# First expert results handed to the second picks' rows, sums scattered straight to the output, dispatch scatters of the attention stage spread

## What is computed

```
logits = xf @ gate_w.T                      # 8192 x 8
top_p, top_i = top_k(softmax(logits), 2)
w = top_p / (sum(top_p) + 1e-9)
capacity = int(1.25 * T / E)                # 1280 rows for each expert and pick
rank = the token's place among those that picked this expert with this pick
y = down(silu(gate(x)) * up(x))             # only where rank < capacity
out = x + w0 * y0 + w1 * y1                 # a pick over capacity adds nothing
```

## Time and profile before

| | |
|---|---|
| median of 3 runs (lowest, highest) | 1113.87 us (1110.75, 1114.72) |
| profiled execution: its time, its span | 1111.77 us, 1110.0 us |
| mean granted TensorE clock | 0.888 |
| busy share: PE, DVE, POOL, ACT | 84%, 55%, 48%, 42% |
| linear attention | 0 to about 280 us |
| cross-attention and routing | about 280 to 803 us, last batch's exponentials at 758 us |
| experts | 804 to 1085 us |
| loading, adding and storing the second picks | 1085 to 1110 us |
| `DMA_INDIRECT` of the attention (L842), of the experts (L1603) | 128 x 1.01 us, 160 x 0.98 us |

### The profile page before, as it was taken

The page is one execution under the profiler, slowest core; times in us unless marked ns, Lnnn a source line. Parts: engine busy times, 40 slices in busy tenths (PEclk is TensorE's granted clock), DMA queues, the critical chain, the costliest instruction groups (busy, mean ns, idle before and its releaser), DMA issues.

```text
span 1110.0 us, 26366 instructions
## 1 busy us (share of the span) xinstructions
PE 930.1 (84%) x9107; PEld 656.8 (59%) x9107; DVE 615.1 (55%) x1940; ACT 466.1 (42%) x722; POOL 537.0 (48%) x747
## 2 busy tenths in 40 slices
PE   4799999999899888889888888896189899899860
PEld 3577777776566565556566566665156566666550
DVE  6788888886467665556566566543212222233336
ACT  1365566664455444444444444442033333233320
POOL 2466565665223444443444444444625666555660
PEclk8799999999999987887799798965589999899995
DMA  6379200000000000000000000000023322335418
GB/s 215 98 279 338 85 0 0 0 1 1 2 3 10 18 17 21 15 10 4 7 7 7 9 9 9 9 22 9 13 72 88 96 81 70 96 97 146 121 36 303
DMA packets 48178, 67.25 MB, mean 61 GB/s; under 512 B 12338, under 2 KB 25441, under 8 KB 48088
## 3 DMA queue, kind: packets, MB, share of 16 engines
q1 hardware_dynamic: 36480, 52.65, 14.6%
q0 software_dynamic: 9216, 8.42, 2.7%
q10 hardware_dynamic: 2392, 4.93, 1.1%
HBM read 34.41 MB, written 42.09 MB: 69 GB/s over the span
## 4 chain that ended last, share of the span: by engine, by line
PE 50%; another core or an unknown queue 14%; issue 6%; DVE 3%; POOL 2%; ACT 2%; DMA 2%; POOLq 0%; DVEq 0%; ACTq 0%; SPq 0%
PE psum L1709 9%; PE psum L1286 8%; PE psum L1272 7%; PE psum L1721 5%; PE psum L1306 5%; PE psum L1260 2%; PE psum L1289 2%; PE psum L1314 2%; DVE Y L1635 1%; PE psum L625 1%; PE psum L1256 1%; PE psum L1703 1%; POOL dispatched L842 1%; PE psum L605 1%
## 5 line engine op out<-in xcount | busy, mean ns | idle before, releaser
L1603 POOL DMA_INDIRECT expert_out<-yo,token x160 | 156.5, 978 | 124.5 <-issue 107.2
L842 POOL DMA_INDIRECT dispatched<-z,idx x128 | 129.0, 1008 | 101.3 <-DVE idx L1027 53.9
L1185 ACT ACTIVATE PT<-psum,key_bias 77x2048 f32<-77x2048 f32 x64 | 125.6, 1962 | 123.0 <-PE psum L1289 112.9
L1646 DVE TENSOR_TENSOR h<-psum,act_g 128x512 f32<-128x512 f32 x80 | 53.5, 689 | 185.4 <-PE psum L1709 105.9
L918 DVE TENSOR_REDUCE top_score<-psum 128x8 f32<-128x616 f32 x128 | 101.8, 795 | 42.6 <-PE psum L1272 38.9
L1286 PE MATMUL psum<-qT,Kb 32*77 32x128 f32 x2048 | 105.6, 326 | 18.6 <-ACT MT L1198 17.5
L1272 PE MATMUL psum<-Kb,qT 32*128 32x308 f32 x512 | 110.1, 508 | 0.8 <-issue 0.5
L1709 PE MATMUL psum<-xT,gate 128*128 128x512 f32 (+1 forms) x192 | 82.9, 564 | 17.5 <-ACT xT L1666 9.2
L1286 PEld LDWEIGHTS psum<-qT,Kb 32*77 32x77 f32 x2048 | 72.8, 173 | 32.0 <-issue 31.2
L1681 ACT ACTIVATE act_g<-psum 128x512 f32<-128x512 f32 x80 | 46.0, 596 | 96.4 <-PE psum L1709 29.6
L1721 PE MATMUL psum<-down,h 128*128 128x128 f32 x640 | 80.8, 280 | 5.1 <-DVE h L1646 5.1
(11 more groups left out here) (169 smaller groups left out, 1766.7 us busy)
## 6 DMA issues: line engine op xcount, KB each, us to landing
dispatched<-zeros SPq DMA_DIRECT2D x40, 258.0 KB, 2.7
xin<-dispatched SPq DMA_DIRECT2D x40, 258.0 KB
expert_out<-zeros SPq DMA_DIRECT2D x32, 256.0 KB, 2.1
X<-in_x SPq DMA_DIRECT2D x16, 256.0 KB, 2.7
yb<-expert_out SPq DMA_DIRECT2D x16, 256.0 KB
Y<-expert_out SPq DMA_DIRECT2D x7, 512.0 KB, 7.9
out<-Y ACTq DMA_DIRECT2D x7, 512.0 KB, 6.6
expert_out<-yo,token POOLq DMA_INDIRECT x160
```

Source lines behind the costliest of these rows:

```text
L842: pool.indirect_dma_start(xg, bass.IndirectOffsetOnAxis(ap=idx[par][:, t, k:k + 1], axis=0), z4[par][:, t, :], None, bounds_check=ROWS - 1 ...
L1185: nc.scalar.activation(PT[j % 2][:], T.rearrange("p a c -> p (a c)"), ACT.Exp, bias=key_bias[:, bass.ds(b, 1)]).then_inc(s["PT_ready"], 1)
L1603: pool.indirect_dma_start(yt[slot], bass.IndirectOffsetOnAxis(ap=token[i][:, t:t + 1], axis=0), yo[i][:, t, :], None, bounds_check=P * B - ...
```

## The change

- Each dispatched row grows from 129 to 261 floats: the normalised row, the token's row of X, its code, the row its first result goes to (`PLACE`), a mark that its second pick was dropped (`ALONE`), and both weights. ACT copies the X rows into `z4` (`residual_side`, one 128x512 copy a group), DVE writes the rest in `route` steps 13 to 16; `W` is gone.
- First results are no longer combined at the end. In slot 0 a group's result is `w0 * y + ALONE * x` and is scattered to the token's place in the second picks' rows (`handed`, a region behind the output's 8192 rows), or to the output where there is no second pick. In slot 1 it is `w1 * y + (x + first)` and goes straight to the output. `first` is loaded in rows' order, for each group of slot 1 (`load_first`). X is stored to the output beforehand (`store_x`), for tokens that no expert takes. The stage from 1085 to 1110 us, its loads, its 64 DVE operations and its stores, and `add_first` are gone.
- Eviction of the down products moves from ACT to DVE: one 128x512 operation (`base`) and four 128x128 ones (L1664 of the new file) ahead of the two products `h` of the next group. The down products go to three banks in turn, so PE may run one group further ahead of the eviction. Rows are loaded three groups ahead in place of two.
- The scatters of the attention are spread: tile 0 at j = 3 behind `split_top`, tile 1 at j = 0 behind `ln_scale`, tile 2 at j = 0 and tile 3 at j = 1, each behind `split_top`. `idx` is made at the end of the turn j = 3.
- Zeros: `dispatched` has twice the bytes, and one buffer of 10240 rows takes the place of two of 8192.

```diff
+
+
+X_AT, CODE, PLACE, ALONE, WEIGHT = P, 2 * P, 2 * P + 1, 2 * P + 2, 2 * P + 3
+ROW = WEIGHT + K2
 OUT_OF_RANGE = 1.0e6
...
+        sems["zeros"] = 16 * (ROWS + E * CAP) // GROUP_ROWS
 
...
+            with sp.Fori(0, E * CAP // GROUP_ROWS) as i:
+                sp.dma_start(handed[bass.ts(i, GROUP_ROWS), :].rearrange("(p a) c -> p (a c)", p=P),
+                             zeros[:, 0:G4 * P]).then_inc(s["zeros_stored"], 16)
 
...
@@ -836,6 +836,7 @@
 
             def scatter(g, par, t):
                 if t == 0:
+                    pool.wait_ge(s["residual_ready"], g + 1)
...
                 for j in range(G4):
                     b = G4 * g + j
                     if j == 0:
+                        if group(g + 2):
+                            ln_scale(g + 2, 3, mom3, var3, rs3, shift3)
                         if group(g - 3):
                             scatter(g - 3, other, 1)
-                        if group(g + 2):
-                            ln_scale(g + 2, 3, mom3, var3, rs3, shift3)
-                    if j == 1 and group(g - 3):
-                        scatter(g - 3, other, 2)
-                        scatter(g - 3, other, 3)
                     if j == 2:
                         if group(g - 1):
                             ln_scale(g - 1, 4, mom4, var4, rs4, shift4)
                         if group(g):
                             add_out_bias(g)
+                    if batch(b + 2):
+                        split_top(b + 2, j % 2)
                     if j == 3 and group(g - 2):
                         scatter(g - 2, par, 0)
-                    if batch(b + 2):
-                        split_top(b + 2, j % 2)
+
+                    if j < 2 and group(g - 3):
+                        scatter(g - 3, other, j + 2)
...
                         dve.wait_ge(s[f"scattered{par}"], 16 * G4 * K2 // 2 * (g - par))
-                    v.scalar_tensor_tensor(idx[par][:], row[:], float(ROWS), drop[:], ALU.add, ALU.add).then_inc(s["idx_ready"], 1)
+
+                    v.tensor_scalar(taken[:], rank[:, :, 1], float(CAP), None, ALU.is_lt)
+                    v.tensor_scalar(z4[par][:, :, ALONE], rank[:, :, 1], float(CAP), None, ALU.is_ge)
+                    v.scalar_tensor_tensor(away[:], row[:, :, 1], float(ROWS - E * CAP + TOKENS) - NO_TOKEN,
+                                           codes[:, bass.ts(g, G4)], ALU.add, ALU.subtract)
                     ins = v.scalar_tensor_tensor(pair[:], total[:], 1e-9, ex[:, :, E], ALU.mult, ALU.add)
...
                 if k == 14:
+                    v.tensor_tensor(away[:], away[:], taken[:], ALU.mult)
                     ins = v.tensor_scalar(pair[:], pair[:], 1.0, None, ALU.add)
                 if k == 15:
-                    ins = v.reciprocal(weight[:, :, 0], pair[:])
+                    v.tensor_tensor(z4[par][:, :, PLACE], away[:], codes[:, bass.ts(g, G4)], ALU.add)
+                    ins = v.reciprocal(z4[par][:, :, WEIGHT], pair[:])
                 if k == 16:
-                    ins = v.tensor_tensor(weight[:, :, 1], weight[:, :, 0], ex[:, :, E], ALU.mult)
-                if k == 17:
-                    ins = v.scalar_tensor_tensor(W[:, bass.ts(g, G4), :], rank[:], float(CAP), weight[:], ALU.is_lt, ALU.mult)
+                    ins = v.tensor_tensor(z4[par][:, :, WEIGHT + 1], z4[par][:, :, WEIGHT], ex[:, :, E], ALU.mult)
                 ins.then_inc(s["step"], 1)
+
+            def indices(g, par):
+                dve.wait_ge(s["step"], STEPS * g + STEPS)
+                v.scalar_tensor_tensor(idx[par][:], row[:], float(ROWS), drop[:], ALU.add, ALU.add).then_inc(s["idx_ready"], 1)
 
...
-                        routed(15, 16, 17)
+                        routed(15, 16)
+                        if group(g - 2):
+                            indices(g - 2, par)
...
                 if t == G4 - 1:
                     ins.then_inc(s["z4_ready"], 1)
...
+            def residual_side(g, par):
+                nc.scalar.activation(z4[par][:, :, X_AT:X_AT + P], X[:, bass.ts(g, G4), :], ACT.Copy).then_inc(s["residual_ready"], 1)
...
                         z4T_side(g - 1)
+                        residual_side(g - 1, other)
 
...
         gate_ps, up_ps = banks[0:2], banks[2:4]
-        tp, y_ps = banks[4], banks[5].rearrange("p (t c) -> p t c", t=G4)
+        tp = banks[4]
+
+        y_ps = [banks[k].rearrange("p (t c) -> p t c", t=G4) for k in (5, 6, 7, 5, 6)]
...
+                    sp.wait_ge(s["y_ready"], n - PAIR + 1)
...
+            def store_x(g):
+                sp.wait_ge(b["x_out"], g + 1)
+                sp.dma_start(rows_out.rearrange("(p b) c -> p b c", b=B)[:, bass.ts(g, G4), :],
+                             X[:, bass.ts(g, G4), :]).then_inc(s["x_stored"], 16)
+
+            def load_first(n, i, p):
+                for k in range(PAIR):
+                    sp.wait_ge(s[f"y{k}_scattered"], 16 * G4 * PAIRS // K2)
+                sp.wait_ge(s["y_ready"], n - PAIR + 1)
+                sp.dma_start(first[i][:], rows_of(handed, n - NE // K2, i)).then_inc(s[f"first{i}_loaded"], 16)
...
-                    if has(n + 2):
-                        load_x(n + 2, (i + 2) % PAIR, p if i + 2 < PAIR else p + 1)
+                    if has(n + 3):
+                        load_x(n + 3, (i + 3) % PAIR, p if i + 3 < PAIR else p + 1)
...
-                    if slot == 1 and i < 4:
-                        g = 4 * (p - PAIRS // 2) + i
-                        for k in range(PAIR):
-                            sp.wait_ge(s[f"y{k}_scattered"], 16 * G4 * PAIRS // K2)
-                        sp.wait_ge(s["x_added"], g + 1)
-                        load_y(g, i)
+                    if slot == 1:
+                        load_first(n, i, p)
...
-            second = yt[1].rearrange("(p b) c -> p b c", b=B)
-            for i, (u, w) in enumerate(stretches):
-                sp.dma_start(Y[:, u:w, :], second[:, u:w, :]).then_inc(s[f"Y{i}_loaded"], 16)
-            sp.wait_ge(s["out_stored"], 16 * len(stretches))
...
+                        pool.indirect_dma_start(rows_out if slot else out, bass.IndirectOffsetOnAxis(ap=token[i][:, t:t + 1], axis=0), yo[i][:, t, :], None,
+                                                bounds_check=TOKENS - 1 if slot else TOKENS + E * CAP - 1, oob_is_err=False).then_inc(s[f"y{i}_scattered"], 16)
+
+            pool.wait_ge(s["x_stored"], 16 * NG)
...
+            def residual(n, i, p, slot):
+                if some(n):
+                    dve.wait_ge(s["y_ready"], n)
+                rows = xin[i][:, :, X_AT:X_AT + P]
+                if slot == 0:
+                    ins = v.tensor_tensor(base[:], rows, over(xin[i][:, :, ALONE], 2, P), ALU.mult)
+                else:
+                    dve.wait_ge(s[f"first{i}_loaded"], 16 * (p - PAIRS // 2) + 16)
+                    ins = v.tensor_tensor(base[:], rows, first[i][:], ALU.add)
+                ins.then_inc(s["base_ready"], 1)
+
+            def y_side(n, i, p, slot):
+                residual(n, i, p, slot)
+                dve.wait_ge(s["base_ready"], n + 1)
+                dve.wait_ge(s["y_ps"], n + 1)
+                for t in range(G4):
+                    last = v.scalar_tensor_tensor(yo[i][:, t, :], y_ps[i][:, t, :], xin[i][:, t, WEIGHT + slot:WEIGHT + slot + 1],
+                                                  base[:, t, :], ALU.mult, ALU.add)
+                last.then_inc(s["y_ready"], 1)
 
             def body(p, slot):
                 for i in range(PAIR):
                     n = PAIR * p + i
+                    if has(n - 1):
+                        y_side(n - 1, (i - 1) % PAIR, p if i else p - 1, slot_of(p, i, slot, -1))
                     for c in range(HC):
                         dve.wait_ge(s["g_ready"], HC * n + c + 1)
                         dve.wait_ge(s["up_ps"], HC * n + c + 1)
@@ -1645,31 +1677,22 @@
                             dve.wait_ge(s["y_ps"], n)
                         v.tensor_tensor(h[:, c, :], up_ps[c], act_g[:, c, :], ALU.mult).then_inc(s["h_ready"], 1)
...
+            i = PAIR - 1
+            residual(NE - 1, i, PAIRS - 1, 1)
+            dve.wait_ge(s["base_ready"], NE)
+            for t in range(G4):
+                dve.wait_ge(s["tile_ps"], t + 1)
+                v.scalar_tensor_tensor(yo[i][:, t, :], banks[t][:, 0:P], xin[i][:, t, WEIGHT + 1:WEIGHT + 2],
+                                       base[:, t, :], ALU.mult, ALU.add).then_inc(s["tile_ready"], 1)
...
-            def y_side(n, i, p):
-                act.wait_ge(s["y_ps"], n + 1)
-                if some(p):
-                    act.wait_ge(s[f"y{i}_scattered"], 16 * G4 * p)
-                nc.scalar.activation(yo[i][:], y_ps, ACT.Copy).then_inc(s["y_ready"], 1)
...
             def project_down(n, i):
                 pe.wait_ge(s["h_ready"], HC * n + HC)
-                if some(n):
-                    pe.wait_ge(s["y_ready"], n)
+                if some(n - 1):
+                    pe.wait_ge(s["y_ready"], n - 1)
```

110 lines of the change are left out of this document (38 added, 72 removed).

## The result

The changed kernel takes **1041.12 us** (median of 4 runs, 1037.2 to 1046.8) beside 1113.03 us before (4 runs, 1110.8 to 1114.7): ratio 0.936, 95% interval 0.931 to 0.941. The profiled execution has a span of 1039.3 us, against 1110.0. The forecast was 1057 us, range 1026 to 1092.

A forecast was written before the change was run, and what follows sets the result against it. POOL's scatters delay PE's signals and the clock then falls; a 24.5 us end stage runs in series. Span 1110.0 - 24.5 - 47 + 3 + 11 + 1 = 1053.5 us, median 1057, range 1026 to 1092.

The forecast's parts named there:

- The spreading: Attention: scatters in pairs instead of bursts shorten groups to 27.6 us; -47 us, bounds 26 and 67 us gain.
- Additions in the attention: Attention: extra DVE and ACT work hidden in idle time, later idx +1.5, wider expert load +1.5; together +3 us.
- Experts: Experts: evictions ahead of h delay it and POOL's start; +11 us, between 0 and +23.
- The switch: Change to second picks: DVE's eviction waits for first, so h comes late; +1 us, bounds -3 and +6.
- The end: Kernel end: the stage behind the last scatter's landing goes, with nothing covering it; -24.5 us.
- The offset: Whole kernel: a profiled span becomes a median time by adding 3.9 us.
- D: Attention rival: signal delay grows with row size, groups take 35.4 us; 1151 us, chance 0.08.
- C: Attention rival: the burst only moves to turn j = 0, only the clock is kept, h pays fully; 1090 us, chance 0.19.
- B: Rival: all attention scatters cost 0.32 us and up products hide the experts' evictions; 1026 us, chance 0.19.
- E: Experts rival: base and POOL's scatters exclude each other, costing POOL 28 us; 1085 us, chance 0.07.
- What was to show it: Expected signs: span ends within 2 us of last landing, groups 26 to 29 us, late num signals 1 to 2 us.
- A sign of being wrong: Attention: the clock falling at turn j = 0 instead of behind j = 1 would make the prediction wrong.

The follow-up runs named there:

- e1_unspread: The changed kernel with POOL's scatters of tiles 1 to 3 back in the old places; 1104.31 us on the first chip.
- e2_spread_only: The kernel before with only POOL's new order of steps in the attention (order alone), nothing else changed; 1045.13 us, ratio 0.940.
- e3_even: The changed kernel with one tile's pair of attention scatters per turn, in place of 2, 4, 2 and 0; 1039.09 us.
- e4_h_first: The changed kernel with DVE's four evictions and base behind the next group's two h products instead of ahead; 1046.63 us.
- f1_switch: The changed kernel with, only at the switch, the eviction that waits for first moved behind h; 952.67 us, ratio 0.985, fourth chip.

## Why the prediction was right, and where it was not

Direction and range held, the forecast was 16 us too high, and it held only where signals come late. With the order-alone kernel as the divide, the five terms come out at -69, +12, +4, +4 and -21 us where -47, +3, +11, +1 and -24.5 were forecast. The errors of -22, +9, -7, +3 and +3, and -2 of the offset, partly cancel, so that the total is as close as 16 us is in part luck.

- **The spreading, -47.** The mechanism was right: late signals of PE under POOL's scatters, and the clock behind them. `e1_unspread` and `e2_spread_only` take the gain away and give it back by POOL's order alone. The size was not right. The order alone gave -68.8 us up to the last scatter of the attention, a little beyond my upper bound of 67. I had assumed that tiles 1 and 2, one `split_top` apart, still act as part of a burst. They don't (`e3_even`): tile 2's pair is free where it stands, and nearly all of what is left is tile 1's pair under the signal for the next exponential. Pricing by scatter, 0.32 or 1.2 us, was the wrong unit. It is better priced by signal: how long one that is needed waits for the end of the scatters over it.
- **Additions in the attention, +3.** Measured +9.3 up to the last scatter and +2.6 to the experts' first, on the first chip. "ACT was idle, DVE was idle: 0" overlooked that ACT and DVE were idle for signals, and that a later `idx` shifts the scatters against PE's signals. That shift is argued from the timelines, not shown apart. About half of the 9.3 is the group of batches 56 to 59 with its half clock. The wider load was near my figure: from the last scatter to PE's first transposes 5.77 us in place of 4.92, 0.9 where I took 1.5.
- **Experts, +11.** A pair of groups with first choices went from (127.08 - 3.84) / 19 x 2 = 13.0 to 13.4 us, and PE's wait for `h` from 5.1 to 23.1 us. But the whole of the 160 scatters grew by 4.2 - 1.3 = 2.9 us, nearer to the lower bound of 0. The step that failed: taking `h` to be late because of the evictions. `e4_h_first` removed just that and gained nothing, as `h` and the evictions wait for the same late signals, 67.1 us in one place and 65.1 + 3.0 in the other.
- **The switch, +1.** Measured +3.3 and, with signals on time, +6.4, just over my upper bound of 6. I had followed `first` up to `h`, rightly (8.49 us of waiting), but not what PE does behind it: 5.7 us idle and then half clock.
- **The end, -24.5.** Measured -20.4. I let the span end with the last scatter's landing, 2.1 us behind its start; it ends 6.2 us behind. What fills the other 4 us no trace here shows.
- **The offset** from span to median was taken as 3.9 us; the changed kernel's is 1.8.
- **The rivals.** D (delay by row size) is out: spread scatters of 1044 and of 516 bytes give groups of 26.8 and 25.7 us, not 35.4. C is out by the clock and the groups, but for the one group where a run of four is left. B named the right size for the spreading. E is out: the scatters grew from 978 to 993 ns and, with signals on time, from 973 to 987, 8 x 0.015 = 0.1 us a pair of groups if it were all `base`'s doing, not 1.4. The 28 us of E came from one item of the Trainium skill, "SBUF — State Buffer", section "Who interferes with whom": a VectorE operation with two SBUF inputs contends with a GpSimd one that reads SBUF. A later item of the same section infers that `tensor_tensor` takes only the read interface of the pair that the two engines share, and that descriptor generation needs the write interface. The prediction didn't weigh that item, and these lengths agree with it.
- **What was to show it:** groups of 26 to 29 us, no half clock behind j = 1 and DVE's wait for `first` came, and `num` waited 16.5 us in 12 waits, 1.4 us each, though once 4.8. The span's end within 2 us of the landing did not. A sign of being wrong, the clock falling at turn j = 0, came in one group, that of batches 56 to 59.
- **What no case held:** that the largest term isn't there on every chip. With signals on time the change is worth 0.5%, just about what a measurement can tell from no change, and its spreading gains nothing. The first row of the chain, 14% under "another core or an unknown queue" for a kernel of one core, was the sign: it could be put down to nothing in the program, and I treated it as a property of the program.

## What to carry over

When a wait is put down to nothing that the program contains, time both kernels on a second chip before building on it: the same order of one queue was worth 63 us on one chip and nothing, or a loss of some us, on others. An order for a queue that holds up others' signals is planned by which signal comes due under each instruction, not by counting instructions. And an idle engine ahead of a product says who released it last, not what to move: put only the operation that waits for a far transfer behind the work that doesn't (`f1_switch`, 5.5 us in the stretch it touches), and leave the others.
